# Attention and mixture-of-experts kernel: batch 0 is started slot by slot, and VectorE alone rotates its first eight heads

## The reference

```python
q, k, v = split(x @ W_qkv)                  # 16 heads x 16 columns each
q, k = rot(q), rot(k)                       # [x1*cos - x2*sin, x1*sin + x2*cos]
att = q @ k.T / sqrt(16) + causal mask
y = (softmax(att) @ v) @ W_o
x = layernorm(x + y)
gate = softmax(x @ Wg + bg); top-2, renormalised
x = layernorm(x + sum_e gate_e * (x @ We[e].T + be[e]))
```

## Time and profile before

| | us |
|---|---|
| median of 3 runs | 3245.92 |
| lowest, highest | 3244.48, 3248.39 |
| the profiled execution | 3247.9 |
| its span in the trace | 3246.2 |
| TensorE busy | 3110.3 (96%) |
| VectorE busy | 2684.6 (83%) |
| ScalarE busy | 1885.3 (58%) |
| GpSimd busy | 1198.2 (37%) |

### The profile page before, as it was taken

One profiled execution on the slowest core, in us unless ns is written; L12 is line 12 of the kernel. 1 busy time (PEld: TensorE's weight loads), 2 busy tenths in 40 slices (PEclk: granted clock), 3 DMA queues, 4 the chain that ended last, 5 costly groups with the idle time before them and its releaser, 6 DMA issues.

```text
span 3246.2 us, 58552 instructions
## 1 busy us (share of the span) xinstructions
PE 3110.3 (96%) x18752; PEld 1712.3 (53%) x18752; DVE 2684.6 (83%) x8456; ACT 1885.3 (58%) x4257; POOL 1198.2 (37%) x1410
## 2 busy tenths in 40 slices
PE   4789999999999999999999999999999999999987
PEld 2234555555555555555555555555555555555555
DVE  6877888888888888888988888888888888888745
ACT  2266556575565656556575665657565565755551
POOL 3153424444243443424344342434324344442110
PEclk8699999999999999999999999999999999999997
DMA  5344324333442434334333442443443243344000
GB/s 134 62 70 81 60 57 77 62 68 66 80 65 50 78 58 79 60 76 65 55 73 61 83 65 57 73 66 68 66 83 60 55 79 61 69 65 70 4 27 14
DMA packets 174819, 210.95 MB, mean 65 GB/s; under 512 B 26008, under 2 KB 124592, under 8 KB 174256
## 3 DMA queue, kind: packets, MB, share of 16 engines
q1 hardware_dynamic: 173056, 202.98, 35.9%
q10 hardware_dynamic: 1456, 4.23, 0.3%
HBM read 138.44 MB, written 67.11 MB: 63 GB/s over the span
## 4 chain that ended last, share of the span: by engine, by line
PE 84%; DVE 8%; issue 3%; ACT 2%; POOL 1%; DMA 1%; ACTq 0%; SPq 0%; DVEq 0%; POOLq 0%
PE bank L917 22%; PE attend L1012 15%; PE scores L990 14%; PE bank L974 14%; PE bank L954 6%; PE bank L1036 3%; PE bank L963 3%; DVE bank L775 2%; PE bank L1020 1%; PE bank L942 1%; DVE maxima L778 1%; PE bank L1027 1%; PE bank L1044 1%; ACT weights L651 1%; PE bank L1068 1%
## 5 line engine op out<-in xcount | busy, mean ns | idle before, releaser
L651 ACT ACTIVATE weights<-scores 128x512 f32<-128x512 f32 (+3 forms) x3072 | 1333.5, 495 | 886.0 <-PE scores L990 872.7
L775 DVE CUSTOM_DVE_ANT_0 bank<-bank,far_q 128x128 f32<-128x128 f32 (+3 forms) x2048 | 963.1, 512 | 202.7 <-PE bank L974 187.2
L974 PE MATMUL bank<-k_stack,q_stack 96*128 96x512 bf16 (+3 forms) x3072 | 803.6, 333 | 31.7 <-DVE maxima L775 10.5
L990 PE MATMUL scores<-q_stack,k_stack 99*128 99x512 bf16 (+3 forms) x3072 | 821.1, 328 | 10.6 <-ACT weights L651 6.9
L571 POOL TENSOR_SCALAR_AFFINE_SELECT weights<-weights 128x512 f32<-128x512 f32 x512 | 325.4, 637 | 1269.4 <-ACT weights L651 1269.1
L778 DVE TENSOR_REDUCE maxima<-bank 128x1 f32<-128x512 f32 x1024 | 643.9, 682 | 71.2 <-PE bank L974 70.9
L1012 PE MATMUL attend<-weights,values 128*32 128x512 f32 (+3 forms) x6144 | 579.2, 492 | 1.0 <-POOL weights L571 0.9
L990 PEld LDWEIGHTS scores<-q_stack,k_stack 99*128 99x128 bf16 x3072 | 280.1, 97 | 411.8 <-ACT weights L651 154.6
L974 PEld LDWEIGHTS bank<-k_stack,q_stack 96*128 96x128 bf16 x3072 | 276.9, 98 | 400.6 <-issue 153.6
L917 PE MATMUL bank<-wexp_hi,zT_hi 128*128 128x512 f32 x1024 | 381.7, 454 | 11.1 <-DVE lowrows L795 11.1
L891 DVE SCALAR_TENSOR_TENSOR z<-bank,picked,z 128x256 f32<-128x256 f32 x512 | 247.5, 483 | 113.8 <-PE bank L917 104.9
(11 more groups left out here) (110 smaller groups left out, 3133.5 us busy)
## 6 DMA issues: line engine op xcount, KB each, us to landing
parts_scratch<-parts SPq DMA_DIRECT2D x128, 384.0 KB, 2.5
q_stack<-parts_scratch SPq DMA_DIRECT2D x384, 128.0 KB, 7.1
k_stack<-parts_scratch SPq DMA_DIRECT2D x384, 128.0 KB, 7.7
x_in<-in_x SPq DMA_DIRECT2D x64, 256.0 KB, 3.6
z<-in_x SPq DMA_DIRECT2D x32, 512.0 KB, 5.3
out<-z SPq DMA_DIRECT2D x32, 512.0 KB, 3.2
q_stack<-lowrows SPq DMA_DIRECT2D x192, 8.0 KB, 2.4
z<-in_w_exp ACTq DMA_DIRECT2D x1, 1024.0 KB, 4.9
```

The source lines that it names most:

```text
L651: act.activation(weights[:, n % NW, hh, c0:CH], st[(QUAD * n + hh) % NS][:, c0:CH], ACT.Exp, scale=DH ** -0.5).then_inc(S["weights_ready"], 1)
L775: dve.tensor_tensor_reduce(out=b[:, 0:w], in0=b[:, 0:w], in1=far_q[:, CH - w:CH], scale=1.0, scalar=-SENTINEL, op0=ALU.add, op1=ALU.max, a ...
L974: pe.matmul(b[:, 0:w], q_stack[0:ROWS, n, hh, qt * P:(qt + 1) * P], k_stack[0:ROWS, n, hh, kc * CH:kc * CH + w], start=True, stop=True).th ...
L990: pe.matmul(st[(QUAD * n + hh) % NS][:, c0:CH], k_stack[0:MROWS, s, hh, kb * P:(kb + 1) * P], q_stack[0:MROWS, s, hh, qc * CH + c0:(qc + 1 ...
```

## The change

**Stages.** There is a new stage `early` between `pre` and `first`, and each stage has an order of its own, written out. `pre` now ends with B of slot 0, its MC and its MT. `early` holds ST.0 to ST.11 and PV.0 to PV.9, that is slot 0's scores and attention, together with the 48 B of slot 1 (they are called B.3.x.y there) and slot 1's MC and MT at its end. `first` starts at ST.12, with the B of slots 2 and 3 and of the next batch's slots 0 and 1 spread over it. `mid`, `last` and `post` have the same steps in the same order as before.

**Banks.** They are numbered in turn in every stage by itself. In `mid` that gives the same numbers as before; in `first`, `last` and `post` the turn is now even.

**Rotation of heads 0 to 7 in `pre`.** VectorE does it all, straight from the PSUM bank, into a part of `weights` that isn't in use yet; both subtractions of their casts are VectorE's too. The copy of these halves by ScalarE is gone. Heads 8 to 15 (s = 1) are rotated and cast by GpSimd as in the other stages, and VectorE only shuffles for them. The split of the expert weights stands ahead of the casts of s = 1, and the first 16 of slot 0's B stand ahead of the last two casts.

```diff
-SEGMENTS = ("pre", "first", "mid", "last", "post")
+SEGMENTS = ("pre", "early", "first", "mid", "last", "post")
+START = ("pre", "early", "first")
...
+EARLY = steps("""
+B.3.0.0 B.3.0.1 B.3.0.2 B.3.0.3 B.3.1.0 B.3.1.1 B.3.1.2
+ST.0.0 ST.0.1 ST.0.2 B.3.1.3 ST.0.3 MASK.0 B.3.2.0
...
+ST.11.0 ST.11.1 ST.11.2 MC.3 ST.11.3 MASK.11 MT.3
+""")
+FIRST = steps("""
+B.0.0.0 B.0.0.1 B.0.0.2 B.0.0.3 B.0.1.0
+ST.12.0 XL.0 XL.1 ST.12.1 ST.12.2 ST.12.3 B.0.1.1 XT.0 XL.2 XT.1 B.0.1.2 MASK.12 PV.10 PV.11 YE.0.1
...
-        out += [("LOAD", 2), ("WSPLIT",)] + scores + [("MC", 0), ("MT", 0)]
-        out += [("B", 1, it, hh) for it in range(ITEMS) for hh in range(QUAD)]
-        out += [("MC", 1), ("MT", 1)]
+        cast = [("CAST", *half, n) for half in halves[:4] for n in range(2)]
+        out += [("QK", *halves[0]), ("ROPE", *halves[0]), ("QK", *halves[1]), ("ROPE", *halves[1]), cast[0]]
+        out += [("QK", *halves[2]), ("ROPE", *halves[2]), cast[1], cast[2]]
+        out += [("QK", *halves[3]), ("ROPE", *halves[3]), cast[3], cast[4], ("QK", *halves[4]), ("ROPE", *halves[4])]
+        out += [cast[5], cast[6], cast[7], ("LOAD", 0), ("WSPLIT",)]
+        cast = [("CAST", *half, n) for half in halves[4:] for n in range(2)]
+        out += [*cast[0:2], ("QK", *halves[5]), ("ROPE", *halves[5]), ("VP", 0), ("VP", 1), *cast[2:4], ("LOAD", 1)]
+        out += [("QK", *halves[6]), ("ROPE", *halves[6]), ("VP", 2), ("VP", 3), ("QK", *halves[7])]
+        out += scores[:8] + cast[4:6] + [("ROPE", *halves[7])] + scores[8:16] + cast[6:8] + [("LOAD", 2)] + scores[16:]
+        out += [("MC", 0), ("MT", 0)]
...
-    for seg in ("mid", "pre"):
-        steps = [s for s in plan(seg) if s[0] in BANKED]
-        for n, step in enumerate(steps):
-            out["pre" if seg == "pre" else "run", step] = n % NB
+    for seg in SEGMENTS:
+        for n, step in enumerate(s for s in plan(seg) if s[0] in BANKED):
+            out[seg, step] = n % NB
...
+def on_vector(seg, step):
+
+    return seg == "pre" and step[1] == 0
...
+        def half_of(c, s, k):
+
+            return weights[:, 0, k] if on_vector(c.seg, ("ROPE", s, k)) else rope[:, k % 2]
...
+                elif kind == "QK" and on_vector(c.seg, step):
+                    return
...
+                elif kind == "ROPE" and on_vector(c.seg, step):
+                    s, k = a
+                    qk, x1, ch = ("QK", s, k), half_of(c, s, k), k // 2
+                    n = bank(c.seg, qk)
...
+                    dve.stream_shuffle(rope_swap[:, :], bk[n][:, :], SWAP).then_inc(S["swapped"], 1)
+                    dve.tensor_tensor(x1, bk[n][:, :], cos[:, ch * CH:(ch + 1) * CH], ALU.mult).then_inc(free[n], 1)
+                    dve.wait_ge(S["swapped"], c.at("swapped", step))
+                    dve.tensor_tensor(rope_swap[:, :], rope_swap[:, :], sin[:, ch * CH:(ch + 1) * CH], ALU.mult) \
+                       .then_inc(S["sines"], 1)
...
+                    dve.tensor_tensor(x1, x1, rope_swap[:, :], ALU.add).then_inc(S["rotated"], 1)
```

242 lines of the change are left out of this document (168 added, 74 removed).

## The result

| | before | after |
|---|---|---|
| median (lowest, highest), 6 runs each | 3247.32 (3244.48, 3251.60) us | 3238.01 (3233.29, 3238.95) us |
| profiled execution, its span | 3247.9, 3246.2 | 3238.0, 3236.3 |
| mean granted clock of TensorE | 0.979 | 0.983 |

The ratio is 0.9964, with a 95% interval of 0.9954 to 0.9974: the kernel became 9.3 us faster. I had forecast 3211 us, 35 us faster, with a range of 3196 to 3227. The direction was right. The size was wrong, and the time lies outside the range. The six runs after lie in two groups, two at 3233.3 to 3233.9 and four at 3238.0 to 3239.0 us, so two medians of a few runs each that differ by less than 5 us are not told apart by that alone.

A forecast was written before the change was run, and what follows sets the result against it. Repeated stages were taken as full on TensorE, with time to win at the ends: 34.2 us by the end of `first` plus 1.2 from banks, off 3247.9, less 2.0 to the median, gave 3211 us, range 3196 to 3227.

The forecast's parts named there:

- The start of batch 0: In `pre`, VectorE's rotation gets slot 0's load out 6 us earlier and its MT done 15.5 us earlier, at 92.1.
- the 3.5 that I took: Between slot 0's MT and the first ST: three DMAs issued and landed in 3.5 us, first ST at 95.6.
- slot 2's load: On SP's queue ahead of slot 0's row DMAs; at worst 3 us of delay, nothing charged.
- The split beside GpSimd: Expert weights' split in `pre`: 7.1 us undisturbed plus 3.2 us for blocking by GpSimd, ending at 55.5 us.
- Rival C: Start of batch 0 gets no faster, as its chain only changes hands; first maximum at 75, 3222 us; chance 0.17.
- `early` and `first` together: From first ST to end of `first`: 150.6 us of TensorE work, 160.2 plus a 2 us wait, ending 34.2 us earlier.
- I take 0.94: TensorE's busy share over `early` and `first`, chosen between 0.91 of old `first` and 0.99 of the repeated stage.
- The 139.7: TensorE's busy us in the old `first`, taken as base for both new stages with the starting low clock included.
- rival D: TensorE stays at the low clock through `early` and perhaps part of `first`, making the kernel slower, up to 3255; chance 0.03.
- 2.0 at ST.12: At the start of `first`, TensorE stands 2 us waiting for slot 1's maxima to come through MT and three DMAs.
- The work of the 48 B: Slot 1's maxima tiles added beside the attention: 12.6 us of TensorE work to a slot.
- the 1.2 us where I had them: Even turn of the banks in `last` and `post`: 1.2 us off, between 0 and 4.

The follow-up runs named there:

- split_only: Kernel before, plus even banks and the change's new stages and orders, with the old rotation kept; 3248.90 us, ratio 0.9997.
- banks_only: Kernel before, with only the PSUM banks numbered in turn in every stage; 3242.68 us, ratio 0.9980.
- rot_only: The change, with slot 1's maxima back behind slot 0's in `pre` and the old order of `first`; 3224.64 us, ratio 0.9924.
- b48_more: New rotation, even banks, old stages, next batch's x loaded sooner; against that, 48 tiles in `first` made and reduced twice; 3240.71 us, ratio 0.9968.
- rows_sooner: The change, with slot 1's last two B, MC and MT placed six to seven ST sooner in `early`; 3232.97 us, ratio 0.9948.
- slot2_alone: New rotation, even banks, old stages, x loaded sooner; against that, slot 2's maxima also taken alone before the first ST; 3245.86 us, ratio 0.9988.

## Why the prediction was wrong, step by step

**The start of batch 0: right.** First maximum 64.2 forecast, 62.4 measured; MT of slot 0 done at 92.1 forecast, 90.2 measured; slot 0's load issued at 46.9, forecast 47.7. The first ST came at 97.0 instead of 95.6, since the rows needed 6.8 us behind MT, and not the 3.5 that I took. Of slot 2's load ahead of them I wrote "at the worst it costs 3 us, and I charge nothing". It cost the worst: 3.3 us. The DMA engines were full until 94 us, and the rows' last DMA took 5.43 us, against 1.91 in split_only. The product from a PSUM bank took 0.69 us, the value taken. The gain came through whole: 17.4 us at MT of slot 0, and 18.0 in the median from banks_only to rot_only.

**The split beside GpSimd: right in size, not in place.** 9.1 us measured, 10.3 forecast. I had expected subtractions above 2.29 us. They took 2.29 both; instead both 128x8 copies took 1.12 us, each ending within 0.03 us of the end of a GpSimd subtraction (46.44 and 48.61), while before the second had taken 0.16 with GpSimd idle. Ahead of the split, VectorE's subtraction at 41.02 took 1.60, where 0.69 is usual. That fits the rule of the Trainium skill ("SBUF — State Buffer", "SBUF: two separate sides") that one of the two is shut out while the other works. The long subtractions started only after GpSimd was done, so these rows don't test it on them, and no run shows by which part of the rule a copy with one input is held. Rival C, a start that isn't faster, is refuted.

**`early` and `first` together: the step that failed.** I wrote "Together 150.6 us" of TensorE work and "I take 0.94", 162.2 us with the wait at ST.12. It was 185.1, with 162.5 us busy and a share of 0.88. The trace gives the 22.9 us of error as 11.9 more busy and 11.0 more idle:

- *Busy, 11.9 us.* The stretch ran 22.4 us at the low level. The 139.7 held 4.2: before's 2.3 behind the first ST and the 1.9 of the transposes ahead of it (138.4 to 140.3, clock 0.50). Three ST of 99x512 in a row took 1.46 us at the low level (96.99) and 0.81 at the high one (111.51). Taken as half the speed, the 18.2 us more are some 9 us of busy time. My sentence "The low clock at the start is in the 139.7 already" was the slip: the 139.7 held 4.2 us at the low level, and I took the same for a start that has another order and other work around it. Why the old order reached the full level so soon isn't shown. In the change TensorE stays at 0.51 for 12.5 us after the first ST, although it is busy 12.45 of them, and is low again from 136.7, around ST.12, and at 249 (windows of the change):

```profile
136.70:143.50 6.80, 6.58 (x36) 3.55 (x37) 0.98 (x4) 4.30 (x9) 0.63 (x1) 0.52 0.49 147
...
249.00:252.40 3.40, 3.40 (x15) 0.82 (x15) 2.13 (x11) 1.08 (x2) 0.12 (x1) 0.51 0.55 166
```

  The Trainium skill has the price ("TensorE: Matmul & The Clock Gate", "HAM oscillation — how this bites in real kernels"): the extra time is the time at the low level times one half. The rows agree: 1.46 against 0.81 us for the same three matmuls, and 11.9 us more busy, of which this price explains 9; the other 3 aren't placed. This is rival D's mechanism, to which I gave 0.03 as an all-or-nothing case; it came as a part of it.
- *Idle, 11.0 us.* I had 9.6 idle and 2.0 at ST.12. About 5.6 us come with the 48 tiles themselves, as b48_more shows without any of the change's start. Another 4.1 are the two stands at slot 1's rows (1.25 and 2.82), where I had 2.0. In rows_sooner, with slot 1's transpose moved forward, the stage has 1.9 us less idle time. The remaining 3 us or so I can't place.

The work of the 48 B was sized well, 12.6 us forecast for all of them, 13.5 measured in b48_more, with 3.2 us more at the low level in them. What was wrong in kind was the view of the stage. I read TensorE's 91% in `first` before as room of 9%, and the 99% of the repeated stage as a share that this mix could come near. The first attention stage had nearly the same length with 144 and 192 B (some 5 us apart at an equal clock), and the next 48 cost their work in full and 40% on top (19.1 us against 13.5). The Trainium skill warns of this reading ("Perfetto Trace Analysis", "Identifying the Most-Contended Engine": the busy share of matmuls is not a good measure of how close one is to the roofline, as they are pipelined). slot2_alone agrees: 48 fewer B took only 3.8 us off the busy time, or some 8 at an equal clock, where by their mean time they are 12.6. I should have put the marginal cost of a tile, and not the share, into the sum.

**The balance of the part by slots.** Taking slot 1's maxima beside slot 0's attention saves the 26.5 us stretch that they had alone, less what the start loses elsewhere: the first ST comes 25.4 us earlier. It pays 19.1 us for 48 tiles above the knee. It would still have won 6.3. To the 19.1 come, by estimate, some 8 us for the low clock (half of 22.4 - 6.7), 4.1 for the two stands, and 6.4 that make up the 37.6; of these, 1.9 are the transposes of x, which in rot_only stood ahead of the first ST, and the rest isn't placed. Together it is a loss of 12.2 us in the traces, 13.4 in the medians.

**Banks: a gain is shown, but not the 1.2 us where I had them.** I had them in `last` and `post`. banks_only gave 6.9 in the median of 11 runs against 21: in its trace the first ST comes 1.2 us earlier, the stage is 2.7 shorter, and what lies behind it is 2.5 us shorter. The 1.2 can't be the banks' doing, as `pre` has the same banks in both kernels. Behind `first` the change itself took 2955.9 us, exactly as before did; banks_only and rot_only have 2953.5, and all kernels with the even banks 2951.6 to 2957.5. So only the 2.7 us in the stage are placed, and no trace shows my term.

**What remains open.** What sets the length of 147 to 148 us of the attention stage below the knee isn't isolated. In the 20 us of slot2_alone without maxima, TensorE is busy 16.8 and ScalarE 14.4 us, and neither is full. The two take turns at the score banks; that this is the bound is a guess. Nor was a start by slots tried with fewer maxima in `first`, since there is nowhere else to put them.
